# Two decoder layers on one core: modulation products, first transposes, shared products and late weight loads in other places

## What is computed

```python
mod = (_silu(L0_c) @ L0_wmod).reshape(L0_c.shape[0], 6, 1, -1)
sa, ca, ga, sb, cb, gb = (mod[:, 0], ..., mod[:, 5])
gb = (2 * (gb >= 0) - 1) * jnp.maximum(jnp.abs(gb), 0.25)      # ga in the same way
h = _layernorm(x, axis=-1) * (1 + ca) + sa
x = x + ga * _L0_attn_ref(h, ...)                              # RWKV recurrence over each sequence
h = _layernorm(x, axis=-1) * (1 + cb) + sb
x = x + gb * _L0_ffn_ref(h, ...)                               # router: 6 of 32 experts, and a shared expert
```

## Time and profile before

| | us |
|---|---|
| median of 3 runs | 437.58 |
| lowest, highest | 435.03, 437.88 |
| the profiled execution | 438.39 |
| its span, first to last instruction | 436.6 |

### The profile page before, as it was taken

How to read it: one execution, slowest core, us unless ns; L and a number is a source line. 1 busy time by engine, 2 the same in 40 slices (tenths; PEclk the granted TensorE clock), 3 DMA queues, 4 the chain that set the end, 5 groups by cost and what they waited for, 6 DMA issues and landing times. The chain is left out here.

```text
span 436.6 us, 6170 instructions
## 1 busy us (share of the span) xinstructions
PE 407.1 (93%) x1923; PEld 306.7 (70%) x1924; DVE 286.3 (66%) x693; ACT 201.8 (46%) x380; POOL 129.3 (30%) x143
## 2 busy tenths in 40 slices
PE   6996898988999999999999899899899979999997
PEld 6463748455777777777776647687587858798886
DVE  4898885887444444444444476989677998985542
ACT  2578825482222222222222247482896397613430
POOL 1000020004777777777777500701000010010000
PEclk9999696968999999999999989999999989999999
DMA  8996667981323233333238259902400000001001
GB/s 278 413 389 135 149 148 179 360 373 41 104 98 107 98 108 96 107 96 110 96 106 276 87 189 376 359 12 44 172 2 0 2 1 0 2 2 48 2 0 49
DMA packets 24010, 56.89 MB, mean 130 GB/s; under 512 B 4528, under 2 KB 15794, under 8 KB 22996
## 3 DMA queue, kind: packets, MB, share of 16 engines
q1 hardware_dynamic: 18564, 41.80, 28.7%
q0 software_dynamic: 5424, 14.82, 10.3%
HBM read 46.10 MB, written 10.50 MB: 130 GB/s over the span
## 5 line engine op out<-in xcount | busy, mean ns | idle before, releaser
L736 PE MATMUL bank<-arena,tile_mem 128*128 x224 | 75.6, 460 | 0.0
L1411 POOL DMA_INDIRECT tile_mem<-h_dram,gidx x57 | 56.0, 982 | 53.8 <-DVE gidx L1779 36.8
L1399 POOL TENSOR_TENSOR rstd<-ve,mhalf 128x2 f32<-128x2 f32 (+1 forms) x14 | 11.3, 806 | 185.9 <-DVE ve L1539 185.9
L1418 POOL DMA_INDIRECT y_dram<-norm,didx x56 | 55.3, 988 | 21.8 <-issue 13.7
L1795 DVE TENSOR_TENSOR tile_mem<-tile_mem,bank 128x176 f32<-128x176 f32 x56 | 18.9, 338 | 62.3 <-ACT tile_mem L1209 62.3
L752 PE MATMUL bank<-arena,tile_mem 88*128 x224 | 57.7, 379 | 0.8 <-DVE tile_mem L1790 0.8
L752 PEld LDWEIGHTS bank<-arena,tile_mem 88*128 88x128 f32 x224 | 42.4, 190 | 15.7 <-issue 1.0
L847 PE MATMUL bank<-x_r,f_r 128*128 128x512 f32 x192 | 46.4, 402 | 0.7 <-DVE x_r L1975 0.6
L736 PEld LDWEIGHTS bank<-arena,tile_mem 128*128 128x128 f32 x224 | 38.3, 191 | 11.8
L1209 ACT ACTIVATE tile_mem<-bank 128x176 f32<-128x176 f32 x56 | 17.8, 317 | 57.5 <-PE bank L736 57.5
L847 PEld LDWEIGHTS bank<-x_r,f_r 128*128 128x128 f32 x192 | 36.8, 193 | 9.8 <-issue 0.8
(11 more groups left out here) (281 smaller groups left out, 722.0 us busy)
## 6 DMA issues: line engine op xcount, KB each, us to landing
arena<-w_gu SPq DMA_DIRECT2D x3, 2112.0 KB, 12.3
arena<-w_dn SPq DMA_DIRECT2D x4, 1408.0 KB
arena<-w_gu SPq DMA_DIRECT2D x2, 2464.0 KB, 20.5
arena<-y_dram SPq DMA_DIRECT2D x6, 768.0 KB, 8.2
arena<-w_f SPq DMA_DIRECT2D x6, 512.0 KB, 7.8
arena<-wmod SPq DMA_DIRECT2D x3, 512.0 KB, 9.3
arena<-wmod SPq DMA_DIRECT2D x2, 768.0 KB, 11.0
arena<-y_dram SPq DMA_DIRECT2D x4, 384.0 KB, 4.5
```

Of the source, the lines that this page charges most:

```text
L736: mm = pe.matmul(bank[2 + r % 2][:, 0:2 * M], xgT[r % 2][:, k * P:(k + 1) * P], gu[:, bass.ds(e[k], 2 * M)], start=(k == 0), stop=(k == CT ...
L1411: pool.indirect_dma_start(out=xg[j % 4], out_offset=None, in_=h2_dram, in_offset=bass.IndirectOffsetOnAxis(ap=gidx[:, j:j + 1].bitcast(U32 ...
L1418: pool.indirect_dma_start(out=y_dram, out_offset=bass.IndirectOffsetOnAxis(ap=didx[:, j:j + 1].bitcast(U32), axis=0), in_=yt[j % 4], in_of ...
```

## The change

- `mod_rows` is called for one row at a time: row 0 after the first transposed weights, row 1 after the second, row 2 after the first projection. Rows use banks 2, 5 and 4 and wait for the scans that free these. `mod_cols` moves ahead of the second projection, and 12 products of the identity with itself (`keep_busy`) follow it.
- The second projection is split after two tiles, and the transposes of sequence 0 stand between its halves.
- On ScalarE the sigmoid table is loaded ahead of the first `keep_x`, and the second `keep_x` moves ahead of the second modulation.
- The shared products of the first two token tiles stand one by one after one-hots 10, 15, 20, 25, 30 and 35.
- The feed-forward gate is floored on [2, 256] before it goes through DRAM; the floor on [128, 512] goes.
- The late expert weights: 15 experts (in three loads, those that lie past X) wait for `proj_done` only, the other three for `x1_out`.

```diff
-MOD_BANKS = 4, 7, 4
+MOD_BANKS = 2, 5, 4
+SHARED_AT = (9, 14, 19, 24, 29, 34)
...
+        PAST_X = EARLY + -(-NT * C // GUW)
...
-            sp_.wait_ge(gbraw_ready, 1)
+            sp_.wait_ge(gbraw_ready, 2)
             sp_.dma_start(modg_dram, gb_raw).then_inc(mod_out[0], 16)
...
+            sp_.wait_ge(proj_done, B)
+            for e in range(PAST_X, E, 5):
+                sp_.dma_start(gu[:, e * GUW:(e + 5) * GUW], w_gu[:, e * GUW:(e + 5) * GUW]).then_inc(gu_late, 16)
             sp_.wait_ge(x1_out, 16 * B)
-            for e in range(EARLY, E, 6):
-                sp_.dma_start(gu[:, e * GUW:(e + 6) * GUW], w_gu[:, e * GUW:(e + 6) * GUW]).then_inc(gu_late, 16)
+            sp_.dma_start(gu[:, EARLY * GUW:PAST_X * GUW], w_gu[:, EARLY * GUW:PAST_X * GUW]).then_inc(gu_late, 16)
...
-                    pe.wait_ge(*((sig_ready, CT + 1), (sig_ready, CT + 2), (modrow_ready, 1))[n])
+                    pe.wait_ge(*((exparg_ready, CT + 1), (exparg_ready, CT + 2), (sig_ready, CT + 1))[n])
...
-            def project(b, banks):
+            def project(b, banks, between=None):
 
                 for t in range(TB):
+                    if t == 2 and between:
+                        between()
...
-            for b in range(B):
-                gated_weights(b)
+            gated_weights(0)
+            mod_rows(range(1))
+            gated_weights(1)
+            mod_rows(range(1, 2))
             pe.wait_ge(wg_ready, B)
             preload_x(0, RES_BANKS[0])
             pe.wait_ge(yT_ready, CT)
             project(0, RES_BANKS[0])
-            pe.wait_ge(exparg_ready, CT + 1)
+            mod_rows(range(2, 3))
+            pe.wait_ge(modrow_ready, 1)
             pe.wait_ge(v_used, CT + 1)
             preload_x(1, RES_BANKS[1])
-            mod_rows(range(3))
+            mod_cols((SA, CA, SB, CB), modrow1, 3, 4)
+            pe.wait_ge(sig_ready, CT * B)
+            keep_busy(12, bank[7][:, 0:P])
             pe.wait_ge(yT_ready, CT * B)
-            project(1, RES_BANKS[1])
-            mod_cols((SA, CA, SB, CB), modrow1, 3, 4)
+            project(1, RES_BANKS[1], lambda: transposes(B, 0, None, LN2_BANKS[0]))
...
-                transposes(B + b, b, (x_done, b) if b else None, LN2_BANKS[b])
                 if b:
+                    transposes(B + b, b, (x_done, b), LN2_BANKS[b])
...
-                t, k = divmod(n, TOPK)
-                if k == TOPK - 1 and t in (2, 5):
-                    if t == 2:
-                        pe.wait_ge(shhid_ready, SHT)
-                    shared_out(0, (2, 3), range(t // 3, t // 3 + 1))
+                if n in SHARED_AT:
+                    t, k = divmod(SHARED_AT.index(n), SHT)
+                    if t == 0:
+                        pe.wait_ge(shhid_ready, k + 1)
+                    shared_product((2, 3), t, k)
...
+            act.preload_act_table(ACT.Sigmoid)
             keep_x(0)
...
             token_scores(0)
+            keep_x(1)
             modulated(3, 1, 0, SB, CB, LN2_BANKS[1])
...
             token_scores(1)
-            keep_x(1)
...
             exponents(2)
+            dve.wait_ge(gbraw_ready, 1)
+            gate_floor(gb_raw, gb_tmp[0], gb_tmp[1], gbraw_ready, gb_raw)
             outputs(0)
...
-            dve.wait_ge(modB_in[0], 16 * B)
-            gate_floor(*[v.rearrange("p t c -> p (t c)") for v in (gb0[:, :, :], norm[:, TB:TB + 2, :], norm[:, TB + 2:NT, :])])
-            settle()
```

18 lines of the change are left out of this document (11 added, 7 removed).

## The result

The changed kernel takes 435.15 us (median of 20 runs, 432.91 to 439.26) against 438.56 us for the kernel before (20 runs, 433.50 to 441.86). The medians differ by 3.4 us (0.8%). The ratio on record is 0.9945, with a 95% interval of 0.9918 to 0.9971, a gain of 0.55%: real, but smaller than the 1% named in the prediction, whose forecast was 434.5.

A forecast was written before the change was run, and what follows sets the result against it. VectorE up to 60 us, then a path zigzagging between engines, was taken to bound the first 106 us, which alone could move. 2.6 + 0.8 - 0.3 = 3.1 us off a median of 437.58 gave 434.5 us; range 431.6 to 437.8.

The forecast's parts named there:

- Up to the second projection: Ahead of the second projection: products fit TensorE's pauses, the clock stays at 2.4 GHz, projection starts at 58.9, 1.2 us earlier.
- The gate's floor: Feed-forward gate floored on 2x256 in VectorE's 2.07 us pause: 1.5 us estimated, hidden, at worst 0.3 us late.
- The split: Second projection: ScalarE modulates sequence 0 while TensorE projects; router products run from 63.7 instead of 67.14, 3.4 us earlier.
- Half of the shared expert's first half at half clock: Ahead of the rank products: half these products at half speed, ranks start about 78.2, 2.6 us earlier (1 to 4.5).
- The gate of the row stores: Start of the one-hots: both row stores must land, behind the down weights, at 84.0; gain at most 2.75 us.
- Rival 3: Row stores slip past the down weights and don't wait: 7.1 us gained, 430.5 us; chance 0.05.
- The one-hots: VectorE's stalls of 2.59 us among the one-hots: 0.8 us taken as gain, 0.3 us lost to the last shared products.
- Late weights: Issued right behind the last row store, in by 102.7 when the first tile starts: 0 to 0.3 us.
- only the first 106 us can move: From about 107 us on, expert tiles and the second layer keep TensorE busy; the change touches none of that code.
- Rival 2: Half clock from the router products through the shared expert's first half: about 0.4 us gained, 437.2 us; chance 0.14.
- Rival 1: TensorE stays at 2.4 GHz to the end of the one-hots: 5.3 us gained, 432.3 us; chance 0.23.
- Rival 4: Row stores share engines with the late weights, the last landing about 96: some 7 us lost, 445 us; chance 0.08.

The follow-up runs named there:

- no split: Changed kernel with sequence 0's transposes behind the whole second projection instead of between its halves: 433.26 us, ratio 0.9886 to the kernel before.
- no singles: Changed kernel with the shared products in blocks of three again: 436.3 us, ratio 0.9970 to the kernel before.
- more filler: Changed kernel with two more fillers on TensorE among the router products (8 and 4 products of 128x128): 434.94 us, ratio 0.9895 to the kernel before.
- order alone: Changed kernel with the old gate floor, old late weights and old blocks of three put back: 437.48 us, ratio 0.9954 to the kernel before.
- weights first: Changed kernel with three late weight loads issued ahead of the second row store instead of behind it: 446.19 us, ratio 1.0155 to the kernel before.
- the changed kernel's second measurement: Changed kernel run again with no edit, for a second profile: 433.86 us, ratio 0.9887 to the kernel before.
- old floor: Changed kernel with the gate's floor back behind the store, on the 128-partition copy: 433.83 us, ratio 0.9909 to the kernel before.

## Why the prediction was right, point by point

**Up to the second projection: right.** The products in the pauses held the clock (1.00 at 44), VectorE no longer stops at 53, and the second projection began at 58.24 (58.9 forecast). The filler took 2.94 us (2.7). That the filler helps was half right: it holds the clock where it stands, but without it there are two shorter falls in place of one long one, and the time is the same.

**The gate's floor: right.** It took 1.36 us (1.5 estimated), hidden; the old floor's removal is worth nothing, as forecast. The down weights went out at 35.80 (36.9), because the two-row store between is short: its successor was issued 1.16 us after it.

**The split: the place nearly right, the cause mostly wrong.** Router products at 62.68 (63.7) and the second choice at 72.48 (72.9) came about as forecast, but the step put 2.2 of its 3.4 us (all but the projection's 1.2) down to ScalarE modulating while TensorE projects. Without the split the router products still start at 63.78. Of the 4.5 us measured the earlier start of the projection gives 1.8, the column products that moved ahead of it 0.6, the split 1.4, and a shorter pause the rest; none of the 1.4 shows in the time.

**Half of the shared expert's first half at half clock: as forecast.** Ranks stood at 78.72 (78.2), the products took 5.19 us (half of 3.67 at half speed makes 5.5). It was luck that one number held: in the run without singles, with the same text up to there, ranks stood at 75.75. The stated span of 1 to 4.5 us by the clock was the right way to put it.

**The gate of the row stores: right in kind, 1 to 2 us too late.** 84.0 was forecast; where nothing else was later, the stores released the one-hots at 81.9 to 83.1 (no split, no singles, more filler). In the changed kernel they were issued at 69.8 and 75.0 and landed 7.0 to 8.8 us later, by 83.8 at the latest, and the one-hots at 84.64 waited for nothing: the sign "released by the row stores" did not show. Rival 3 (the stores do not wait) is refuted by the same rows.

**The one-hots: mis-sized.** The 0.8 us taken for the single products was 2.76 in the profiles (15.31 to 12.55), above the 2.6 of the stops alone. The step took half clock up to 102, from the window of before; after, it was down for some 3.4 us only (0.87 over the 13 us from 85 to 98). At one and the same fall of the clock the single products are worth 1.35 us (order alone, 13.90 to 12.55); the rest comes with the shorter fall, which no run shows to be the change's doing.

**Late weights: right, with the cover known now.** They cost nothing at 98.0. With 1.4 MB more in the queue they cost 6.6 us. Their new place was put back only together with other parts (order alone); there they were in by 97.0, 5 us ahead of the first transposes at 101.98, so it is not shown to gain anything either.

**Sum.** In the two profiles the head gained 4.9 us, not 3.1; the first tile's transposes came at 100.57 where 102.5 was forecast. But one pair of profiles does not price the change: the last one-hot sum stands at 94.4 to 100.4 with the new order (weights first aside) and at 97.7 to 102.1 with the old one. The medians show 3.4. That this is so near the sum is in part luck: the one-hots gave 2 us more than forecast, and the end of the tile loop, which the sum left at nothing, took some back. The base was off as well: 437.58, of three runs, against 438.56 of twenty. That the rest of the head's gain goes at the end of the tile loop in part of the executions fits the table, but the table has one execution of each kernel, so the share is not shown. The step "only the first 106 us can move" failed for the profiled execution: the loop's end lost 4.4 us behind a gather wait of 2.61 us instead of 1.04. Rival 2 (it falls longer) happened in its first half, 66 to 77, but not in its price, since the last shared products came in time. Rival 1 (the clock holds, 432.3) did not happen; the run nearest to it, more filler, held the clock at the routers, ran into the row stores and was no faster, but there too the clock fell among the one-hots, so the rival itself stays untried. Rival 4's price was near (446.19 measured with the order reversed, 445 given), and its mechanism did not occur, since the stores stand first in the queue. The Trainium skill (DMA: Bandwidth & Descriptors, Queues, rings and completion order) has descriptors of one ring consumed in order; both runs that exchanged stores and weights agree, 21.3 us to land behind the late weights and 3.3 ahead of the last down weights.

No variant is shown to be better than the changed kernel. The lowest median, 433.26 without the split, has the ratio 0.9886; the changed kernel's second measurement has 0.9887.

## What to carry to other kernels

When a head has several gates that open within 3 us of each other (here the clock, the row stores and the late weights), taking one away gains only the distance to the next, and each must be priced with the others already gone. Follow a gain to the end of the kernel: a stage whose length does not depend on its start passes it on nearly whole, and its last wait can eat it. Where single executions of one kernel take 433 or 441 us, compare the same stretch over several profiles before a stop is put down to an edit.

## What was not expected of the hardware

**In the tile loop GpSimd needs more time per tile than TensorE**, although TensorE is shown busy at 98% there (119.36 of 122 us over 100 to 222 in the changed kernel). GpSimd:

```profile
149.07 0.99 POOL L1433 DMA_INDIRECT y_dram<-norm,didx  x1 [0.30 <-issue]
150.37 0.97 POOL L1426 DMA_INDIRECT tile_mem<-h_dram,gidx  x1 [0.30 <-issue]
151.64 0.99 POOL L1433 DMA_INDIRECT y_dram<-norm,didx  x1 [0.30 <-issue]
```

TensorE in the same stretch:

```profile
151.84 0.39 PE L743 MATMUL bank<-con,tile_mem 128*128 128x128 f32 x2
...
154.33 0.39 PE L743 MATMUL bank<-con,tile_mem 128*128 128x128 f32 x2
```

A scatter and a gather take GpSimd 2.57 us (149.07 to 151.64), with 0.30 us between any two and no other wait from 109 to 240 us; a tile takes TensorE 2.49. So TensorE gains 0.08 us a tile on the gathers: from a gather's issue to the tile's transposes it is 8.63 us at the seventh tile and 4.49 at the 49th. GpSimd's steady pace explains why the stretch between the gathers is nearly the same in all kernels. It does not explain the stop: just ahead of it the lead is 4.62 us in the changed kernel and 4.68 in the kernel before, and the stops are 2.61 and 1.04. What sets their length stays open.

**The clock can come back at very different times in the same instructions**: at 69 us in two executions (no singles, old floor), at 77 in three others (both profiles of the changed kernel, order alone), after a fall near 66 in all five. Which it is decides 3 us. What decides it stays open.
